# Feed-forward groups 2 to 4: the first product in three bf16 passes over exact parts of its input, inputs turned one step sooner

## The chip, the cores and the metric

One NeuronCore of a Trainium2 chip runs the whole program. The metric is the device time in microseconds of one execution. The kernel before was timed in 3 runs.

## What is computed

The input x is 16 images of 96 channels of 16 by 16 pixels, f32. The reference, cut to what matters:

```python
x = x + depthwise_conv_11x11(group_norm(x))                  # stage A
t = to_tokens(x)                                              # 16 x 256 tokens x 96 channels
t = t + attention(layer_norm(t))                              # 6 heads of 16, causal, rotary
t = t + ffn(layer_norm(t))
x = from_tokens(t)

def ffn(x, W1, b1, W2, b2):          # W1: 384 x 96, W2: 96 x 384
    h = bitlinear(x, W1, b1)
    h = gelu(h)                      # exact
    return bitlinear(h, W2, b2)

def bitlinear(x, W, b):
    Wb = sign(W - mean of its fifth of the rows)             # 5 row groups, the rest stays 0
    y = x @ Wb.T + b
    for g in range(5):               # 5 groups of 3 images; image 15 stays 0
        gamma = max(abs(y[g]))
        y[g] = clip(y[g] * 128 / (gamma + 1e-5), -128 + 1e-5, 128 - 1e-5)
    return y
```

Each group of 3 images (768 tokens) has one maximum over all of its hidden values and one over all of its outputs, and nothing behind a maximum can be scaled before it is known.

## The kernel before, in words

The program is written by hand, engine by engine: each engine's function lists its instructions in the order in which they are issued, and semaphores hold an instruction until others are done. There is no scheduler. An engine takes its instructions strictly in that order, so whatever stands behind a waiting instruction waits too.

Stage A (normalisation, convolution, projection to q, k, v) fills the first third. Then `step_b(n)` runs the attention, one image per step on every engine. The part of a step that matters here is on VectorE: `normalise_o`, a first row maximum (`maxima(n + 3, 0)`, L1028), `add_attention`, a second one (`maxima(n + 3, 1)`), and at the end of the step whatever small work on the feed-forward weights and statistics is due (`weight_sums`, `centre_w1`, `centre_w2`, `second_stats`).

The feed-forward stage begins inside the last steps with group 0 and then runs a loop over n = 1 to 4, in which all engines work on neighbouring groups. For a group g the work is this. GpSimd normalises the 768 tokens (`second_rstd`, L502, and `second_norm`, L511 and L514) into `x2_ring`, two groups deep. TensorE turns them to channel-major with six transposes (`transpose_x2`, L1567), part 0 (512 tokens) and part 1 (256 tokens). ScalarE copies each part from PSUM to `x2t_ring` (`channel_major`, L726); a row of ones below it carries the bias. TensorE makes the first product, three blocks of 128 hidden values for each part (`first_product`, L1583), f32, in two instructions each. VectorE reduces each block to its maximum (`largest_hidden`, L1141), and over `hidden_partial` (L1148), TensorE's `hidden_row` (L1590), `hidden_top` (L1154) and TensorE's `hidden_all` (L1595) every partition gets the group's maximum; `hidden_bounds` (L1132 to L1135) makes the clip limits, `clip_hidden` (L1182, L1187, L1191) clips, and ScalarE's `gelu` (L737) scales and applies the GELU. TensorE makes the second product (`second_product`, L1710), ScalarE adds the bias (`output`, L744), VectorE takes the output's maximum (`output_max`, L1196), and over `output_row` (L1742), `output_top` (L1206), `output_all` (L1746) and `output_bounds` the limits of the output come out. GpSimd clips (`limit_output`, L535), TensorE turns the residual (`residual`, L1731), and VectorE scales and adds (`scaled_output`, L1237), after which SyncE stores.

In round n TensorE issues the first product of group n, with the residual and the output maximum of group n - 2 between its blocks, then the second product of group n - 1 with the hidden maximum of group n and the transposes of group n + 1 between its blocks. ScalarE's round is output(n-1) part 0, channel_major(n+1) both parts, output(n-1) part 1, gelu(n) both parts. GpSimd's list behind the last attention step is: rstd and norm of group 3, rstd and norm of group 4, then the clips of the outputs of groups 0 to 4. Both parts of groups 2 to 4 are turned in the same PSUM bank (7), so part 1 waits until part 0 has been copied:

```python
def channel_major(g, part):
    act.wait_ge(s_x2t, 2 * g + part + 1)
    wait(act, s_f1, 2 * HC * (g - 1))
    n = SPANS[part].stop - SPANS[part].start
    nc.scalar.copy(x2t_ring[0:C, g % 2, SPANS[part]], bank[0:C, x2_bank(g, part), 0:n]).then_inc(s_x2c, 1)
```

## Time and profile before

| | us |
|---|---|
| median of 3 runs | 260.1 |
| the three runs | 256.66, 260.1, 261.04 |
| the profiled execution's own time | 258.36 |
| its span, first to last instruction | 256.6 |
| TensorE busy over the span | 230.8 (90%) |
| VectorE busy | 200.4 (78%) |
| ScalarE busy | 139.4 (54%) |
| GpSimd busy | 104.6 (41%) |

Durations and start times below come from one profiled execution and are microseconds from the span's start. An instruction's duration overlaps the next one's start where they are pipelined, so what an instruction costs on its engine is the distance between two starts. `[x <-ENGINE name Lnn]` at a row's end is idle time of the engine before that row and what ended it. PE is TensorE, DVE VectorE, ACT ScalarE, POOL GpSimd.

### The profile page before, as it was taken

The numbers are of one execution on the slowest core, as the hardware profiler recorded it, in microseconds if no ns is written. First come the engines' busy times: TensorE is split into PE (matmuls) and PEld (weight loads), VectorE is DVE, ScalarE is ACT, GpSimd is POOL, SyncE is SP. The second block draws the span as 40 slices with busy tenths as digits, with TensorE's granted clock in tenths as the row PEclk, the third lists the DMA queues.
The fourth block names the chain that finished last, engine by engine and source line by source line (L and its number), as shares of the span: only waits on it lengthen the run. The fifth ranks groups of instructions, "written<-read, shape, count | busy, mean of one in ns | idle before, by whom it ended". The sixth has DMA issues, their size and how long they took to land.

```text
span 256.6 us, 5459 instructions
## 1 busy us (share of the span) xinstructions
PE 230.8 (90%) x1864; PEld 176.8 (69%) x1864; DVE 200.4 (78%) x530; ACT 139.4 (54%) x324; POOL 104.6 (41%) x125
## 2 busy tenths in 40 slices
PE   7779989999999768789999998898998899999981
PEld 7679879899899645567877776676765545545450
DVE  3888988899896985677867777777485978888965
ACT  0351466586565466546876667667747524516250
POOL 2201358557556546433542224467365404010101
PEclk9799999999999999979999999999999999999995
DMA  3990000000699990443443545410000000101103
GB/s 100 251 318 1 0 0 3 1 0 4 103 115 118 119 102 0 84 95 76 86 103 94 94 97 95 92 32 4 0 3 1 3 0 0 46 12 37 46 0 107
DMA packets 24188, 15.68 MB, mean 61 GB/s; under 512 B 3069, under 2 KB 23522, under 8 KB 24162
## 3 DMA queue, kind: packets, MB, share of 16 engines
q1 hardware_dynamic: 22560, 14.06, 30.8%
q10 hardware_dynamic: 1602, 1.29, 2.2%
q8 instruction: 15, 0.25, 0.4%
q14 instruction: 11, 0.09, 0.2%
HBM read 4.26 MB, written 1.57 MB: 23 GB/s over the span
## 4 chain that ended last, share of the span: by engine, by line
PE 65%; DVE 19%; DMA 5%; issue 4%; ACT 2%; SPq 2%; POOL 1%; DVEq 0%; ACTq 0%
PE bank L1351 11%; PE bank L1583 7%; PE bank L1710 7%; PE bank L1461 6%; PE bank L1526 5%; DVE nmax L1028 5%; PE bank L1373 4%; PE bank L1464 4%; DVE xs_ring L891 3%; PE bank L1494 3%; PE bank L1362 3%; DMA stack<-nmax_t 3%; PE bank L1529 2%; DMA cst<-in_const 2%; PE bank L1475 2%
## 5 line engine op out<-in xcount | busy, mean ns | idle before, releaser
L1028 DVE TENSOR_REDUCE nmax<-bank 128x3 f32<-128x384 f32 x64 | 45.5, 752 | 20.6 <-PE bank L1464 20.5
L671 ACT ACTIVATE pt_ring<-bank 128x384 f32<-128x384 f32 x96 | 42.0, 491 | 20.2 <-PE bank L1496 19.6
L483 POOL TENSOR_SCALAR_AFFINE_SELECT pt_ring<-pt_ring 128x512 f32<-128x512 f32 x48 | 31.6, 660 | 49.8 <-ACT pt_ring L671 49.5
L1351 PE MATMUL bank<-xs_ring,toep 128*128 128x192 f32 x256 | 46.6, 328 | 1.0 <-DVE xs_ring L891 1.0
L1351 PEld LDWEIGHTS bank<-xs_ring,toep 128*128 128x128 f32 x256 | 41.8, 190 | 2.5 <-issue 1.2
L1461 PE MATMUL bank<-stack 96*128 96x128 bf16 x192 | 31.7, 250 | 4.3 <-DVE nmax L1028 3.0
L1464 PE MATMUL bank<-mask,ident 128*128 128x128 bf16 x192 | 31.6, 223 | 0.0
L450 POOL TENSOR_TENSOR parts<-rest_ring,parts 96x512 bf16<-96x512 f32 x16 | 18.7, 1171 | 22.3 <-ACT parts L603 22.3
L1461 PEld LDWEIGHTS bank<-stack 96*128 96x128 bf16 x192 | 18.6, 99 | 10.4 <-issue 6.4
L1494 PE MATMUL bank<-stack 97*128 97x256 bf16 x96 | 23.2, 277 | 1.3 <-DMA stack<-nmax_t 1.1
L1710 PE MATMUL bank<-parts,w_b 128*96 128x512 f32 (+1 forms) x60 | 23.1, 492 | 0.2 <-ACT parts L737 0.2
L1583 PE MATMUL bank<-parts,w_b 97*128 97x256 f32 (+1 forms) x60 | 23.2, 500 | 0.0
L443 POOL TENSOR_TENSOR rs_ring<-qk_ring,cst 128x384 f32<-128x384 f32 x16 | 18.1, 1134 | 5.4 <-ACT qk_ring L587 5.3
L1526 PE MATMUL bank<-pt_ring,v_ring 128*32 128x256 f32 x192 | 20.0, 387 | 0.0
L1496 PE MATMUL bank<-stack 97*128 97x128 bf16 x96 | 19.4, 220 | 0.0
L1464 PEld LDWEIGHTS bank<-mask,ident 128*128 128x128 bf16 x192 | 19.0, 99 | 0.2
L744 ACT ACTIVATE parts<-bank,b_s 96x512 f32<-96x512 f32 (+1 forms) x10 | 5.8, 575 | 23.6 <-PE bank L1710 23.4
L1373 PE MATMUL bank<-wa,lt_ring 96*128 96x288 f32 x64 | 18.5, 412 | 0.0
L587 ACT COPY qk_ring<-bank 128x384 f32<-128x384 f32 x16 | 7.7, 479 | 19.0 <-PE bank L1373 19.0
L957 DVE TENSOR_TENSOR qr_ring<-rc_ring,rs_ring 128x384 f32<-128x384 f32 x16 | 14.3, 896 | 2.1 <-POOL rs_ring L443 1.5
L891 DVE TENSOR_TENSOR xs_ring<-bank,cw_bc 128x384 f32<-128x384 f32 x32 | 15.6, 554 | 0.5 <-PE bank L1341 0.5
L1141 DVE TENSOR_REDUCE amax<-bank 128x1 f32<-128x512 f32 (+1 forms) x23 | 14.3, 636 | 1.4 <-PE bank L1583 1.2
(153 smaller groups left out, 470.7 us busy)
## 6 DMA issues: line engine op xcount, KB each, us to landing
stack<-parts SPq DMA_DIRECT2D x96, 96.0 KB, 3.6
tok<-in_x_tok SPq DMA_DIRECT2D x4, 384.0 KB, 12.0
out<-xs_ring SPq DMA_DIRECT2D x4, 288.0 KB, 2.6
stack<-in_x ACTq DMA_DIRECT2D x2, 384.0 KB, 8.7
stack<-nmax_t SPq DMA_DIRECT2D x32, 1.5 KB
stack<-in_x SPq DMA_DIRECT2D x2, 192.0 KB, 4.5
stack<-in_x SPq DMA_DIRECT2D x1, 384.0 KB, 11.0
cst<-in_const SPq DMA_DIRECT2D x1, 384.0 KB, 11.0
```

The source lines that it names most:

```text
L483: nc.gpsimd.affine_select(out=v, in_=v, compare_op=ALU.is_ge, fill=0.0, base=0, pattern=[[0, 2], [0, 2], [1, P]], channel_multiplier=-1).t ...
L671: nc.scalar.activation(pt_ring[:, b % 2, h, :], bank[:, 3 + h % 2, 0:T + P], ACT.Exp, scale=float(HD) ** -0.5).then_inc(s_exp, 1)
L891: last = nc.vector.tensor_tensor(xs_ring[:, s, p].rearrange("p t b c -> p (t b) c"), src, w, ALU.mult)
L1028: last = nc.vector.tensor_reduce(nmax[:, b % 2, k:k + 3], bank[:, 0:3, first:first + (t + 1) * P], op=ALU.max, axis=AX.X, negate=True)
L1351: last = nc.tensor.matmul(dst, w, xs_ring[:, s, p, k].rearrange("p b c -> p (b c)"), start=(k == 0 and p == 0), stop=(k == NT - 1 and p == ...
L1373: last = nc.tensor.matmul(bank[:, 5 + t, 0:3 * C], lt_ring[:, n0 % 2, (2 * u + t) * P:(2 * u + t + 1) * P], wa[:], start=True, stop=True)
L1461: nc.tensor.matmul(bank[:, h % 3, first:first + size], stack[0:KROWS, slot, h, 0, t * P:(t + 1) * P], stack[0:KROWS, slot, h, 1, 0:size], ...
L1464: last = nc.tensor.matmul(bank[:, h % 3, first + t * P:first + size], ident16[:], mask16[:], start=False, stop=True)
L1494: nc.tensor.matmul(bank[:, 3 + e, P:P + T], stack[0:KROWS + 1, slot, h, 1, 0:P], stack[0:KROWS + 1, slot, h, 0, :], start=True, stop=True)
L1526: nc.tensor.matmul(bank[rows, 7, g * T:(g + 1) * T], w, pt_ring[:, s, h, P:P + T], start=True, stop=False)
L1583: nc.tensor.matmul(dst, w1_b[:, k * P:(k + 1) * P], x2t_ring[:, g % 2, SPANS[part]], start=True, stop=True).then_inc(s_f1, 1)
L1710: m = nc.tensor.matmul(bank[0:C, 5 + part, 0:n], w2_b[:, k, :], h_ring[:, g % 2, k, SPANS[part]], start=(k == 0), stop=(k == HC - 1))
```

## The change

Groups 0 and 1 stay as they are. For groups 2 to 4 the f32 input of the first product is split into three bf16 parts that add up to it (`x2_16`): the rounded value, the rounded rest, and the rest of that. The sign weights, which are exact in bf16, are copied to `w1_16`, with three more rows that hold the bias in three bf16 parts against three rows of ones. TensorE makes each block in three bf16 passes (L1583 becomes three instructions).

The parts come from a chain over three engines: ScalarE copies each turned part twice, once to f32 and once to bf16 (`channel_major`); GpSimd subtracts (`rest_x2`, in place); ScalarE rounds the rest to bf16 (`middle_x2`); GpSimd subtracts again (`third_x2`). The first product of the group waits for all of it. To make room, the input of group n + 2 and no longer of n + 1 is turned in round n, and that of group 2 ahead of the loop. The bias parts are made by VectorE in attention steps 7 to 12 and placed by two transfers of SyncE, ScalarE makes `w1_16` in step 10, and VectorE writes the ones in step 5.

The diff, cut to its core:

```diff
+        w1_16 = sb("w1_16", [C + 3, HID], BF16)
...
+        x2_16 = parts[0:C + 3, n_used:n_used + 6 * GT].rearrange("p (s k n) -> p s k n", s=2, k=3)
...
+            sp.wait_ge(s_b1, 4)
+            for k in range(2):
+                sp.dma_start(w1_16[C + 1 + k:C + 2 + k, :], b1_parts[:, k, :]).then_inc(s_b1rows, 16)
...
+            def rest_x2(g):
+
+                pool.wait_ge(s_x2c, 2 * g + 2)
+                v = x2t_ring[0:C, g % 2, :]
+                nc.gpsimd.tensor_tensor(v, v, x2_16[0:C, g % 2, 0, :], ALU.subtract).then_inc(s_x2r, 1)
...
+            def third_x2(g):
+
+                pool.wait_ge(s_x2p1, g - 1)
+                nc.gpsimd.tensor_tensor(x2_16[0:C, g % 2, 2, :], x2t_ring[0:C, g % 2, :], x2_16[0:C, g % 2, 1, :],
+                                        ALU.subtract).then_inc(s_x2p2, 1)
...
             second_rstd(3)
             second_norm(3)
+            rest_x2(2)
+            third_x2(2)
             second_rstd(4)
             second_norm(4)
-            for g in range(QGROUPS - 2):
+            rest_x2(3)
+            third_x2(3)
+            limit_output(0)
+            rest_x2(4)
+            third_x2(4)
+            for g in range(1, QGROUPS - 2):
...
+                if n == 10:
+                    act.wait_ge(s_wsign, 1)
+                    nc.scalar.copy(w1_16[0:C, 0:QGROUPS * W1_ROWS], w1_b[0:C, 0:QGROUPS * W1_ROWS]).then_inc(s_w16, 1)
...
-                nc.scalar.copy(x2t_ring[0:C, g % 2, SPANS[part]], bank[0:C, x2_bank(g, part), 0:n]).then_inc(s_x2c, 1)
+                src = bank[0:C, x2_bank(g, part), 0:n]
+                last = nc.scalar.copy(x2t_ring[0:C, g % 2, SPANS[part]], src)
+                if g >= 2:
+                    last = nc.scalar.copy(x2_16[0:C, g % 2, 0, SPANS[part]], src)
+                last.then_inc(s_x2c, 1)
...
+            def middle_x2(g):
+
+                act.wait_ge(s_x2r, g - 1)
+                nc.scalar.copy(x2_16[0:C, g % 2, 1, :], x2t_ring[0:C, g % 2, :]).then_inc(s_x2p1, 1)
...
+            channel_major(2, 0)
+            channel_major(2, 1)
+            middle_x2(2)
             for n in range(1, QGROUPS):
                 output(n - 1, 0)
                 if n + 1 < QGROUPS:
-                    channel_major(n + 1, 0)
-                    channel_major(n + 1, 1)
+                    if n + 2 < QGROUPS:
+                        channel_major(n + 2, 0)
+                        channel_major(n + 2, 1)
                     output(n - 1, 1)
+                    if n + 2 < QGROUPS:
+                        middle_x2(n + 2)
...
+                    nc.vector.memset(w1_16[0:C, QGROUPS * W1_ROWS:HID], 0.0)
                     nc.vector.memset(w2_b[:, :, QGROUPS * W2_ROWS:C], 0.0).then_inc(s_wready, 1)
+                if n == 5:
+                    nc.vector.memset(x2_16[C:C + 3, :, 0, :], 1.0).then_inc(s_xrows, 1)
+                if n == 7:
+                    nc.vector.tensor_copy(w1_16[C:C + 1, :], w1_b[C:C + 1, :]).then_inc(s_b1, 1)
+                if n == 10:
+                    dve.wait_ge(s_b1, 1)
+                    nc.vector.tensor_tensor(b1_rest, w1_b[C:C + 1, :], w1_16[C:C + 1, :], ALU.subtract).then_inc(s_b1, 1)
+                if n == 11:
+                    dve.wait_ge(s_b1, 2)
+                    nc.vector.tensor_copy(b1_parts[:, 0, :], b1_rest).then_inc(s_b1, 1)
+                if n == 12:
+                    dve.wait_ge(s_b1, 3)
+                    nc.vector.tensor_tensor(b1_parts[:, 1, :], b1_rest, b1_parts[:, 0, :], ALU.subtract).then_inc(s_b1, 1)
                 if n in (8, 9, 13):
                     second_stats({8: 0, 9: 1, 13: 2}[n])
...
-                    wait(pe, s_out, 2 * (g - 3) + 1)
+                    wait(pe, s_out, 2 * (g - 4) + 1)
...
-                nc.tensor.matmul(dst, w1_b[:, k * P:(k + 1) * P], x2t_ring[:, g % 2, SPANS[part]],
-                                 start=True, stop=True).then_inc(s_f1, 1)
+                if g < 2:
+                    nc.tensor.matmul(dst, w1_b[:, k * P:(k + 1) * P], x2t_ring[:, g % 2, SPANS[part]],
+                                     start=True, stop=True).then_inc(s_f1, 1)
+                    return
+                pe.wait_ge(s_x2p1, g - 1)
+                pe.wait_ge(s_x2p2, g - 1)
+                for piece in range(3):
+                    rows = slice(0, C + 3 if piece == 0 else C)
+                    last = nc.tensor.matmul(dst, w1_16[rows, k * P:(k + 1) * P], x2_16[rows, g % 2, piece, SPANS[part]],
+                                            start=(piece == 0), stop=(piece == 2))
+                last.then_inc(s_f1, 1)
...
-                    pe.wait_ge(s_x2c, 2 * min(g + 3, QGROUPS))
+                    pe.wait_ge(s_x2c, 2 * min(g + 4, QGROUPS))
...
+            transpose_x2(2, 0)
+            transpose_x2(2, 1)
+            pe.wait_ge(s_w16, 1)
+            pe.wait_ge(s_xrows, 1)
+            pe.wait_ge(s_b1rows, 32)
             for n in range(1, QGROUPS):
...
-                if n + 1 < QGROUPS:
-                    transpose_x2(n + 1, 0)
+                if n + 2 < QGROUPS:
+                    transpose_x2(n + 2, 0)
...
                 second_product(n - 1, 1, 0)
                 second_product(n - 1, 1, 1)
-                if n + 1 < QGROUPS:
-                    transpose_x2(n + 1, 1)
+                if n + 2 < QGROUPS:
+                    transpose_x2(n + 2, 1)
                 second_product(n - 1, 1, 2)
```

What stands on GpSimd behind the last attention step, before (L502 and L511 to L514 are rstd and norm of a group, L535 and L542 the clips of the outputs):

```order
L514 TENSOR_TENSOR xs_ring<-xs_ring,ln_rstd 128x576 [waits s_x2m]
L502 TENSOR_TENSOR ln_rstd<-ln_var,mhalf 128x6 [waits s_l2var]
L511 TENSOR_TENSOR xs_ring<-tok,ln_mean 128x576 [waits s_x2t,s_l2rstd]
L514 TENSOR_TENSOR xs_ring<-xs_ring,ln_rstd 128x576 [waits s_x2m]
L535 TENSOR_SCALAR parts<-parts,lim 96x768 [waits s_sc2] x3
L542 TENSOR_SCALAR parts<-parts,lim 96x256 [waits s_sc2] x2
```

and in the changed kernel (L564 is `rest_x2`, L569 `third_x2`, L518 rstd, L527 and L530 norm, L551 and L558 the clips):

```order
L564 TENSOR_TENSOR parts<-parts 96x768 [waits s_x2c]
L569 TENSOR_TENSOR parts<-parts 96x768 [waits s_x2p1]
L518 TENSOR_TENSOR ln_rstd<-ln_var,mhalf 128x6 [waits s_l2var]
L527 TENSOR_TENSOR xs_ring<-tok,ln_mean 128x576 [waits s_x2t,s_l2rstd]
L530 TENSOR_TENSOR xs_ring<-xs_ring,ln_rstd 128x576 [waits s_x2m]
L564 TENSOR_TENSOR parts<-parts 96x768 [waits s_x2c]
L569 TENSOR_TENSOR parts<-parts 96x768 [waits s_x2p1]
L551 TENSOR_SCALAR parts<-parts,lim 96x768 [waits s_sc2]
L564 TENSOR_TENSOR parts<-parts 96x768 [waits s_x2c]
L569 TENSOR_TENSOR parts<-parts 96x768 [waits s_x2p1]
L551 TENSOR_SCALAR parts<-parts,lim 96x768 [waits s_sc2] x2
L558 TENSOR_SCALAR parts<-parts,lim 96x256 [waits s_sc2] x2
```

The rest and third of group 2 now stand ahead of the rstd and norm of group 4, those of group 3 ahead of the first output's clip, and those of group 4 ahead of the second's.

TensorE at the seam to the loop, before (the last block of group 1's first product, then the second product of group 0):

```order
L1583 MATMUL bank<-parts,w_b 128x512 [waits s_clip1,s_x2c]
L1710 MATMUL bank<-parts,w_b 96x512 [waits s_h,s_o,s_on]
L1590 MATMUL bank<-ident,gmax 1x128 [waits s_gm1]
L1710 MATMUL bank<-parts,w_b 96x512 [waits s_h]
L1595 MATMUL bank<-top,ones 128x1 [waits s_top1]
```

and in the changed kernel, where L1651 is the first product, L1634 the transposes, L1786 the second product, L1666 `hidden_row` and L1671 `hidden_all`:

```order
L1651 MATMUL bank<-parts,w_b 128x512 [waits s_clip1,s_x2c]
L1634 MATMUL bank<-ident,xs_ring 96x128 [waits s_x2,s_x2c,s_o,s_on]
L1634 MATMUL bank<-ident,xs_ring 96x128 x3
L1634 MATMUL bank<-ident,xs_ring 96x128 [waits s_x2c,s_x2]
L1634 MATMUL bank<-ident,xs_ring 96x128
L1786 MATMUL bank<-parts,w_b 96x512 [waits s_b1rows,s_h,s_xrows,s_w16]
L1666 MATMUL bank<-ident,gmax 1x128 [waits s_gm1]
L1786 MATMUL bank<-parts,w_b 96x512 [waits s_h]
L1671 MATMUL bank<-top,ones 128x1 [waits s_top1]
```

Six transposes have come between the first product of group 1 and everything behind it; the two of part 1 wait for ScalarE's copies of part 0.

## Rows read from the trace of the kernel before

**Rows 1.** Busy time by engine in two stretches: one round of the loop, and the tail.

```profile
211.78:222.47 10.69, 10.64 (x43) 5.60 (x42) 9.25 (x22) 4.39 (x7) 3.15 (x3) 1.00 0.10 28
...
243.33:256.60 13.27, 6.80 (x32) 4.03 (x32) 7.99 (x23) 3.97 (x8) 1.64 (x2) 0.80 0.18 52
```

**Rows 2.** Chain of waits through the feed-forward stage: start, length, what.

```profile
226.33 1.49 PE bank L1583 x6
```

**Rows 3.** Timeline of VectorE in the round of 222.47 to 233.16.

```profile
223.18 0.42 DVE L1196 TENSOR_REDUCE amax<-parts 96x1 f32<-96x256 f32 x1 [0.78 <-ACT parts L744]
...
226.37 0.16 DVE L1132 TENSOR_SCALAR gmax<-bank 96x1 f32<-96x1 f32 x1 [0.19 <-PE bank L1746]
...
228.56 0.74 DVE L1237 SCALAR_TENSOR_TENSOR xs_ring<-parts,lim,bank 96x512 f32<-96x512 f32 x1
...
229.23 0.27 DVE L1154 TENSOR_REDUCE top<-bank 1x1 f32<-1x128 f32 x1
```

**Rows 4.** Timeline of TensorE at the seam and in round 2.

```profile
206.17 1.02 PE L1710 MATMUL bank<-parts,w_b 128*96 128x512 f32 x2
...
207.31 0.27 PE L1590 MATMUL bank<-ident,gmax 128*1 128x128 f32 x1
...
216.97 1.02 PE L1710 MATMUL bank<-parts,w_b 128*96 128x512 f32 x2
...
220.31 0.60 PE L1567 MATMUL bank<-ident,xs_ring 128*96 128x128 f32 x4
...
221.81 0.40 PE L1567 MATMUL bank<-ident,xs_ring 128*96 128x128 f32 x2
```

**Rows 5.** Timeline of ScalarE in round 2.

```profile
221.10 0.57 ACT L726 COPY parts<-bank 96x512 f32<-96x512 f32 x1
...
222.67 0.47 ACT L744 ACTIVATE parts<-bank,b_s 96x256 f32<-96x256 f32 x1
```

**Rows 6.** ScalarE's groups by line and shape (busy, mean ns).

```profile
L603 ACT CAST parts<-rest_ring 96x512 bf16<-96x512 f32 x16 | 9.9, 622 | 2.4 <-DVE rest_ring L923 2.3
...
L726 ACT COPY parts<-bank 96x256 f32<-96x256 f32 x5 | 1.9, 374 | 1.7 <-PE bank L1567 1.7
```

**Rows 7.** Timeline of GpSimd behind the last attention step.

```profile
204.55 1.33 POOL L502 TENSOR_TENSOR ln_rstd<-ln_var,mhalf 128x6 f32<-128x6 f32 x1 [3.16 <-DVE ln_var L1048]
...
211.66 1.15 POOL L511 TENSOR_TENSOR xs_ring<-tok,ln_mean 128x576 f32<-128x576 f32 x1 [5.79 <-PE bank L1567]
...
216.19 0.97 POOL L535 TENSOR_SCALAR parts<-parts,lim 96x768 f32<-96x768 f32 x1 [2.15 <-DVE lim L1135]
```

**Rows 8.** GpSimd's groups by line and shape.

```profile
L450 POOL TENSOR_TENSOR parts<-rest_ring,parts 96x512 bf16<-96x512 f32 x16 | 18.7, 1171 | 22.3 <-ACT parts L603 22.3
```

**Rows 9.** Timeline of VectorE in attention steps 5, 9, 10 and 11.

```profile
136.36 0.44 DVE L1018 TENSOR_REDUCE w_sum<-w_b 128x5 f32<-128x285 f32 x1
...
159.88 1.42 DVE L1028 TENSOR_REDUCE nmax<-bank 128x3 f32<-128x384 f32 x2 [1.39 <-PE bank L1464]
...
162.25 0.23 DVE L1055 RECIPROCAL rsum<-bank 128x12 f32<-128x12 f32 x1
...
166.30 1.42 DVE L1028 TENSOR_REDUCE nmax<-bank 128x3 f32<-128x384 f32 x2 [1.38 <-PE bank L1464]
...
171.99 1.42 DVE L1028 TENSOR_REDUCE nmax<-bank 128x3 f32<-128x384 f32 x2 [0.92 <-PE bank L1464]
```

**Rows 10.** VectorE's groups by line and shape.

```profile
L915 DVE TENSOR_TENSOR rc_ring<-qk_ring,cst 128x384 f32<-128x384 f32 x16 | 11.6, 726 | 1.0 <-ACT qk_ring L587 0.8
...
L796 DVE MEMSET parts<- 1x1536 f32 x1 | 1.3, 1338 | 1.2 <-PEq L1825 1.2
```

**Rows 11.** Timelines of GpSimd and of VectorE, one moment, and VectorE's L1135 without GpSimd.

```profile
197.01 0.64 POOL L483 TENSOR_SCALAR_AFFINE_SELECT pt_ring<-pt_ring 128x512 f32<-128x512 f32 x1 [1.68 <-ACT pt_ring L671]
...
197.16 0.50 DVE L1135 TENSOR_TENSOR lim<-gmax,clip_at 128x2 f32<-128x2 f32 x1
...
219.75 0.14 DVE L1135 TENSOR_TENSOR lim<-gmax,clip_at 128x2 f32<-128x2 f32 x1
```

More of the change, by code:

```diff
@@ L182, in build @@
         y2_ring = wide[0:C, 2 * n_h + 2 * GT:2 * n_h + 4 * GT].rearrange("p (s n) -> p s n", s=2)
+        n_used = 2 * (2 * n_h + 4 * GT)
+        x2_16 = parts[0:C + 3, n_used:n_used + 6 * GT].rearrange("p (s k n) -> p s k n", s=2, k=3)
+        n_used += 6 * GT
+        b1_parts = parts[C:C + 1, n_used:n_used + 2 * HID].rearrange("p (k n) -> p k n", k=2)
+        b1_rest = parts[C:C + 1, n_used + 2 * HID:n_used + 4 * HID].bitcast(F32)
         flat = xs_ring[:, :, :, :, :, :].rearrange("p s q t b c -> p (s q t b c)")
@@ L277, in build @@
         s_x2c = sem("s_x2c")
+        s_w16 = sem("s_w16")
+        s_b1 = sem("s_b1")
+        s_b1rows = sem("s_b1rows")
+        s_xrows = sem("s_xrows")
+        s_x2r = sem("s_x2r")
+        s_x2p1 = sem("s_x2p1")
+        s_x2p2 = sem("s_x2p2")
         s_f1 = sem("s_f1")
```

## The prediction

> **What bounds the kernel now.** I read the busy time by stretch first. In one round of the feed-forward loop (10.69 us) TensorE is busy for 10.64 and VectorE for 9.25, at a granted clock of 1.00, the 2.4 GHz level [rows 1]. The chain of waits names nothing but TensorE there: the six instructions of the first product's part 1 alone stand in it with 1.49 us [rows 2]. Read so far, every 0.1 us taken from the first product would be won. VectorE's timeline says otherwise. In a round it sits idle only where it waits for part 1 of the output, 0.78 us ahead of the row at 223.18, and 0.19 us ahead of the one at 226.37, with a short wait of about 0.25 behind 229.43 [rows 3]. From 223.18 to the end of `hidden_top` at 229.50 it works without a break but for the 0.19. Then TensorE takes over (`hidden_all`, the rest of the second product, transposes), then ScalarE's `output` part 1 at 222.67, then VectorE again at 223.18 [rows 3, 5]. That ring is as long as the round, 10.69, and no first product lies on it. So TensorE and VectorE are balanced to a few tenths, and a faster first product only makes TensorE wait for the maxima.
>
> **The first product.** Three blocks of 512 and three of 256 tokens for each group. The six part-1 instructions take 1.49 us for 3 blocks of 256 [rows 2], less 0.2 of the last one's latency 1.28, so 0.43 a block of 256 and 0.85 a block of 512. f32 in two instructions is four passes if a bf16 pass runs a column in half the time of an f32 instruction; then three passes save a quarter: 3 x 0.21 + 3 x 0.11 = 0.96 us a group, 2.9 over groups 2 to 4. By the ring above only VectorE's 0.19 and some 0.12 between `hidden_top` and `hidden_all` can be won in a round: 0.3 instead of 0.96.
>
> **The seam to the loop.** Before, the second product begins at 206.17 and `hidden_row` of group 1 at 207.31 [rows 4]. Now the four transposes of part 0 come first. A set of four takes 0.60 (row at 220.31), so they end at 206.77. ScalarE then copies and casts the part: 0.57 for the copy (221.10), which starts the cast 0.47 later, and 0.58 for the cast, so 207.85 [rows 5]. Part 1 could start 0.14 behind that, as 221.81 stands to 221.67 now, at 208.0, and the second product at 208.2, two us late. From there `hidden_row` comes at 209.1 instead of 207.31, 1.8 late.
>
> **GpSimd's list is what decides.** It is strictly in order, and four new subtractions of 96x768 are put ahead of work that others need. The trace has no such subtraction. The nearest: 96x512 with a bf16 operand takes 1.171 [rows 8], scaled by elements 1.76, or 1.6 with a fixed 0.2; the f32 one of 128x576 takes 1.15 [rows 7], scaled 1.53. From below, a one-operand operation on 96x768 takes 0.97 [rows 7]; from above I allow 2.3, the 1.76 and the 0.5 of a stall as in rows 11, which here would hit GpSimd. I take 1.65. ScalarE's cast of the rest, 96x768 from SBUF, is 0.62 for 512 [rows 6] plus 0.21 for 256 more: 0.85 with its handover. rstd and norm of a group are 1.33 and two times 1.15 and, with 0.15 of handovers, 3.8 us [rows 7].
>
> Now the walk, on the clock of the old trace. The transposes of part 1 end at 208.4 and ScalarE's two operations (0.37 by rows 6, 0.26 apart) at 209.05. Rest of group 2 to 210.75, cast to 211.65, third to 213.3. Only then come rstd and norm of group 4, which ran from 204.55 when VectorE's statistics were there [rows 7] but are queued behind now: to 217.1. Rest of group 3 to 218.8, cast to 219.65, third to 221.3, clip of output 0 (0.97) to 222.3. Two others wait for this. ScalarE has `gelu(1)` queued behind the cast, so the second product of group 1 starts at 221.25 instead of 216.97 [rows 4]; and VectorE wants the clipped output at 217.88 (a round before 228.56, rows 3) and has `hidden_top(2)` queued behind it. `hidden_top(2)` starts at 223.05 and ends at 223.3, and `hidden_all(2)` is 4.3 us late. That contains the 1.8 of the seam. In round 1 alone the clip of output 0 finished at 217.16 (216.19 plus 0.97, rows 7), 0.7 ahead of its need; that cover is gone.
>
> **Rounds 2 to 4.** In round 2 part 1 of the transposes waits for one more ScalarE operation (+0.5; it starts at 221.81 now, straight behind the copy), and `output` part 1 for a second one (+0.1): 4.9 us late at the row 223.18. VectorE's 0.19 falls away: 4.7. Then comes a wait of another kind. VectorE's small two-operand L1135 took 0.50 instead of 0.14 when GpSimd's L483 ran from 197.01 to 197.65: it ended with it [rows 11]. Now the limits of output 1 (226.6 plus 4.7, so 231.3) meet `third_x2(4)` (rest from 227.7, cast, third from 230.25 to 231.9): +0.5, 5.2 late. In round 3 nothing is turned any more: six transposes and the wait between them, 0.85, leave the ring, 4.2 late, 4.0 behind VectorE's 0.19, and 0.15 once more at `hidden_all(4)`: 3.85 us at the loop's end, carried to the last store.
>
> The Trainium skill, "GPSIMD Engine Reference", section "Elementwise — side-by-side cycle accounting", gives about 2.6 cycles an element for a two-input operation at 1.2 GHz; by an estimate from that page 768 elements are 1.66 us and the sum stays as it is. By a rate in proportion to the f32 row of 576 it would be 1.53, 0.5 less over the walk. No row decides between them.
>
> **The attention steps.** Without extra work a step takes 5.69 us (166.30 to 171.99). With `second_stats`, some 1.0 us of extra work between the maximum that starts at 159.88 and the reciprocal at 162.25, it takes 6.42 (159.88 to 166.30) [rows 9]. So 0.3 of what is added at a step's end is hidden and the rest is paid in full. Step 5 already has a reduction of 0.44 there (136.36) that uses this up. It gets the write of ones, 1536 elements in a partition: the f32 fill of 1536 took 1.338 [rows 10], and I take 1.2 paid; if bf16 fills went four times as fast it would be 0.3. Step 7 has `centre_w2` and gets a cast of 384 elements, one operand against L915's two: I take 0.3 (0.9 with a stall as in rows 11). Steps 10 and 12 get a two-operand subtraction of 384; the same size of L915 took 0.73 on average, some of them stalled [rows 10], and a third of it bounds it from below: I take 0.5, of which 0.2 is paid in step 10 and 0.45 in step 12, where TensorE waits for `normalise_o` as soon as it can run. Step 11's cast hides, ScalarE's copy in step 10 fits into its idle 0.4, SyncE's two transfers come when its list is empty. Sum 2.2 us, between 0.6 and 4.5.
>
> The Trainium skill, "VectorE: DVE Perf Modes", section "Zero memsets can be issued as uint32 (trn2)", says that a fill takes a cycle an element whatever the type, and only fills of zero can be widened; ones in bf16 would then cost what f32 did, and the sum above is kept rather than reduced by 0.9.
>
> **The sum.** 3.85 + 2.2 = 6.05 us. On the profiled execution (258.36, with a span of 256.6) that is 264.4. The median of the runs shown, 260.1, lies 1.7 above it; the forecast on it is 266.2, 2.3% more. A measurement of this kernel can tell about 2% from no change, here 5.2 us.
>
> **Rivals.**
> TensorE bounds throughout, as the chain of waits has it. Then 0.96 a round is won, the seam's 1.8 is eaten up by it in two rounds, and 2.9 remains in all, since the transposes only change their place: 257.2 with the attention's additions hidden as well, 259.4 with them. For it speaks 10.64 of 10.69 us busy, against it VectorE's 9.25. It decides from the point where VectorE gets through a round in 9.7 us and a subtraction takes no more than 0.97, the bound from below. Chance 0.08; even 2.9 is only 1.1% faster.
> The mild case: subtractions cost about 1.15, as if a norm's. The four of the walk save 2.0, it ends at 220.3, and the whole is 260.1 + 4.05 = 264.1, within 2%. If instead the fill of ones is cheap, 265.3. Chance 0.30.
> The forecast, 266.2 with 264.5 to 268: 0.50.
> The clock falls: TensorE now idles from 219 to 221.25, longer than anywhere in the loop before. In the tail, where it is busy for 6.80 of 13.27 us, the granted clock is 0.80 on average [rows 1]. A stretch at 1.2 GHz would double what TensorE does in it, some 2 us: 268.5. Chance 0.12.
>
> So faster by over 2% has 0.03, within 2% 0.43, slower 0.54 (half of the forecast's own range and a little more lies above 265.3, with the clock case). The range is 262.0 to 269.5.
>
> **What would show it.** Right: TensorE idle of over 1 us behind the first transposes, and of some 2 us ahead of the second product of group 1; GpSimd busy without a break from rest 2 to the first clip, 12 to 13 us, its subtractions at 1.6; VectorE waiting over 3 us for the clip of output 0; step 5 of the attention longer by 1.2; rounds 3 and 4 near 10 us. Wrong: no wait for that clip, first products back to back and rounds of 9.8, subtractions under 1.2, or a step 5 of unchanged length.

## The result, and the profile of the changed kernel

| us | before | changed |
|---|---|---|
| median of 4 runs | 260.42 | 273.62 |
| lowest, highest | 256.66, 261.04 | 269.53, 274.31 |
| profiled execution, its span | 258.36, 256.6 | 273.14, 271.4 |
| mean granted clock in it | 0.976 | 0.952 |

The changed kernel is slower: ratio 1.053, 95% interval 1.046 to 1.061, where the forecast was 1.023. All ratios with an interval here leave out runs in which TensorE's clock stayed low for longer; medians hold all runs.

In the feed-forward stage things stand nearly as forecast. GpSimd's and then VectorE's timeline in round 1 of the changed kernel (start, length, engine, line; L564 is `rest_x2`, L569 `third_x2`, L551 the clip of an output, L1202 the limits, L1304 `scaled_output`):

```profile
218.82 1.64 POOL L564 TENSOR_TENSOR parts<-parts 96x768 f32<-96x768 f32 x1 [9.36 <-ACT parts L767]
...
226.74 1.64 POOL L564 TENSOR_TENSOR parts<-parts 96x768 f32<-96x768 f32 x1
229.32 1.64 POOL L569 TENSOR_TENSOR parts<-parts 96x768 bf16<-96x768 f32 x1 [0.94 <-ACT parts L773]
230.94 0.98 POOL L551 TENSOR_SCALAR parts<-parts,lim 96x768 f32<-96x768 f32 x1
```

```profile
227.86 0.53 DVE L1202 TENSOR_TENSOR lim<-gmax,clip_at 96x2 f32<-96x2 f32 x1
...
231.96 0.74 DVE L1304 SCALAR_TENSOR_TENSOR xs_ring<-parts,lim,bank 96x512 f32<-96x512 f32 x1 [1.84 <-POOL parts L551]
```

A subtraction takes 1.64 us (forecast 1.65). From the rest of group 2 to the end of the clip GpSimd takes 13.1 us, as forecast, with two breaks of 0.94 for ScalarE's casts. VectorE's small two-operand L1202 ends with GpSimd's instruction (227.86 + 0.53, 226.74 + 1.64). VectorE waits for the clip, but for 1.84 us and not for the "over 3 us" that the prediction gave as a sign: it already comes later to that point, since part 1 of the output had kept it waiting 1.37 us ahead of 224.58 (0.78 before, [rows 3]) and L1202 took 0.4 longer. The surprise is on TensorE. Its timeline at the same place (L1786 second product, L1666 `hidden_row`), and behind the write of ones in the attention (L1575 the transposed maxima, L1593 the weighted values):

```profile
217.68 0.39 PE L1634 MATMUL bank<-ident,xs_ring 128*96 128x128 f32 x2 [1.25 <-ACT parts L767]
...
230.87 1.38 PE L1786 MATMUL bank<-parts,w_b 128*96 128x512 f32 x2 [2.21 <-ACT parts L784]
232.03 0.42 PE L1666 MATMUL bank<-ident,gmax 128*1 128x128 f32 x1
232.25 1.91 PE L1786 MATMUL bank<-parts,w_b 128*96 128x512 f32 x2
```

```profile
137.92 0.27 PE L1575 MATMUL bank<-ident,nmax 128*12 128x128 f32 x1 [1.71 <-DVE o_norm L1111]
...
138.71 0.63 PE L1593 MATMUL bank<-pt_ring,v_ring 128*32 128x256 f32 x6
...
139.41 1.09 PE L1593 MATMUL bank<-pt_ring,v_ring 128*32 128x256 f32 x6
```

The same six instructions take 0.63 us at 138.71 and 1.09 at 139.41: the clock fell between them. The second product that took 1.02 [rows 4] takes 1.91 at 232.25. The stretches of 4 us with the lowest granted clock between 136 and 236 (stretch, its length, TensorE's busy time and instructions, granted clock, DMA share, GB/s); outside this part, the clock is low at the start (9 to 13) and in the last 2 us:

```profile
136.00:140.00 4.00, 2.29 (x28) 0.92 0.39 94
140.00:144.00 4.00, 4.00 (x33) 0.50 0.48 55
144.00:148.00 4.00, 4.00 (x27) 0.50 0.44 101
148.00:152.00 4.00, 4.00 (x48) 0.80 0.29 52
...
188.00:192.00 4.00, 4.00 (x39) 0.68 0.01 1
...
208.00:212.00 4.00, 4.00 (x34) 0.62 0.02 4
...
232.00:236.00 4.00, 4.00 (x11) 0.64 0.26 74
```

These are four falls (read in steps of 1 us, each goes down to 0.50, the 1.2 GHz level), each behind an idle stretch of TensorE: 1.71 us ahead of 137.92, 1.52 ahead of 186.53, 0.90 ahead of 207.51, 2.21 ahead of 230.87. Not every such stretch is followed by one: behind 1.43 us ahead of 94.64 and 1.25 ahead of 217.68 the clock stays at 1.00. While the clock is at 0.50 TensorE is busy all the time: it has become the bound. In VectorE's timeline the write of ones and the second maxima behind it:

```profile
135.78 1.34 DVE L1154 MEMSET parts<- 3x1536 bf16 x1 [0.38 <-issue]
...
143.42 1.42 DVE L1081 TENSOR_REDUCE nmax<-bank 128x3 f32<-128x384 f32 x2 [1.39 <-PE bank L1531]
```

The second maxima start at 133.62, 143.42 and 151.77, periods of 9.80 and 8.35 us where the kernel before had 6.14 and 6.11. Three explanations were put to the test. Theory A: the additions make TensorE idle, and the clock's falls behind that are what the forecast lacks. Rivals: the additions cost only their own time (B), or the falls have nothing to do with idle stretches (E).

### The profile page after: what moved, and what is told of

Its sections match the earlier page's. It is cut to its first block, busy times and chain, and to the rows that moved or that the text cites. A ratio compares the mean times of both kernels' runs of the same rounds, so it can differ in the third digit from the quotient of the medians.

```text
span 271.4 us, 5539 instructions
## 1 busy us (share of the span) xinstructions
PE 237.2 (87%) x1882; PEld 180.1 (66%) x1882; DVE 204.9 (76%) x536; ACT 144.5 (53%) x334; POOL 115.0 (42%) x131
## 4 chain that ended last, share of the span: by engine, by line
PE 51%; DVE 23%; SPq 6%; issue 6%; POOL 5%; DMA 4%; ACT 4%; DVEq 0%; ACTq 0%; POOLq 0%
PE bank L1418 7%; PE bank L1593 7%; SPq L381 6%; DVE nmax L1081 5%; PE bank L1528 5%; PE bank L1786 4%; PE bank L1561 3%; PE bank L1440 3%; DVE xs_ring L944 3%; PE bank L1531 3%; PE bank L1596 3%; PE bank L1651 2%; DMA stack<-nmax_t 2%; DMA stack<-in_x 2%; PE bank L1542 2%
## 5 line engine op out<-in xcount | busy, mean ns | idle before, releaser
L1528 PE MATMUL bank<-stack 96*128 96x128 bf16 x192 | 32.5, 254 | 4.2 <-DVE nmax L1081 3.0
L1531 PE MATMUL bank<-mask,ident 128*128 128x128 bf16 x192 | 32.4, 225 | 0.0
L1786 PE MATMUL bank<-parts,w_b 128*96 128x512 f32 (+1 forms) x60 | 24.1, 516 | 2.4 <-ACT parts L784 2.4
L1561 PE MATMUL bank<-stack 97*128 97x256 bf16 x96 | 24.1, 286 | 1.0 <-DMA stack<-nmax_t 0.9
L1593 PE MATMUL bank<-pt_ring,v_ring 128*32 128x256 f32 x192 | 21.9, 421 | 0.0
L1563 PE MATMUL bank<-stack 97*128 97x128 bf16 x96 | 20.1, 226 | 0.0
L1786 PEld LDWEIGHTS bank<-parts,w_b 128*96 128x96 f32 x60 | 8.9, 169 | 7.1 <-issue 4.9
```

The source lines that it names most:

```text
L1528: nc.tensor.matmul(bank[:, h % 3, first:first + size], stack[0:KROWS, slot, h, 0, t * P:(t + 1) * P], stack[0:KROWS, slot, h, 1, 0:size], ...
L1531: last = nc.tensor.matmul(bank[:, h % 3, first + t * P:first + size], ident16[:], mask16[:], start=False, stop=True)
L1561: nc.tensor.matmul(bank[:, 3 + e, P:P + T], stack[0:KROWS + 1, slot, h, 1, 0:P], stack[0:KROWS + 1, slot, h, 0, :], start=True, stop=True)
L1563: nc.tensor.matmul(bank[:, 3 + e, 0:P], stack[0:KROWS + 1, slot, h, 1, P:T], stack[0:KROWS + 1, slot, h, 0, P:T], start=True, stop=True).t ...
L1593: nc.tensor.matmul(bank[rows, 7, g * T:(g + 1) * T], w, pt_ring[:, s, h, P:P + T], start=True, stop=False)
L1786: m = nc.tensor.matmul(bank[0:C, 5 + part, 0:n], w2_b[:, k, :], h_ring[:, g % 2, k, SPANS[part]], start=(k == 0), stop=(k == HC - 1))
```

## The experiments

**e1, the ones written elsewhere.**

```diff
-                if n == 5:
-                    nc.vector.memset(x2_16[C:C + 3, :, 0, :], 1.0).then_inc(s_xrows, 1)
+            nc.gpsimd.memset(x2_16[C:C + 3, :, 0, :], 1.0).then_inc(s_xrows, 1)   # GpSimd, at the start
```

> The changed kernel, with the write of ones taken from the end of attention step 5 on VectorE to GpSimd's idle start. Theory A (the 1.34 us write delays TensorE, and the granted clock then falls to 1.2 GHz for some 10 us): both periods of the maxima behind it, 9.80 and 8.35 us now, return to about 6.1, so 5.9 us less, near 267.7. Rival B (only the write's own time is paid, the fall of the clock comes from something else in these steps): 1.2 us less, near 272.4, with the clock still at 0.50 after step 5.

Measured: median 267.91 (264.59 to 268.78), ratio to before 1.038 (1.020 to 1.056). The two periods are 6.15 and 6.11 us, as A has it and B does not. That the median also met A's 267.7 is in part luck. In the profiled execution (5.5 us shorter than the changed kernel's) the two periods give 5.9, the falls behind 1.52 us of idle ahead of 183.77 and 0.89 ahead of 203.43, stretches that it still has, did not come and gave 2.8, and falls at 14 to 21 and at 113 to 116, where the changed kernel's execution had only one at 9 to 13, took back 3.1.

**e2, the ones alone in the kernel before.**

```diff
+                if n == 5:
+                    nc.vector.memset(ones_rows, 1.0).then_inc(s_xrows, 1)
```

> The kernel before with nothing but the same write of ones, 3 partitions of 1536 bf16 values (one stretch instead of two of 768), at the end of attention step 5. Theory A: +5.9 us by the clock's fall in steps 5 and 6, near 266.3, ratio 1.023. Rival B: +1.2, near 261.6, ratio 1.005, clock at 1.00 there.

Measured: four runs between 258.25 and 266.51, median 263.08, between A's number and B's; no verdict. The profiled execution has periods of 9.72 and 8.43 us and a clock of 0.50 from 140 to 148; the run of 258.25 has a mean clock of 0.991. So the same write in the same place is followed by a fall in one execution and not in another. The kernel before has both kinds too: beside these kernels its runs were at 256.5 to 257.4 with a mean clock of 0.987, or at 260.6 to 262.9 with 0.970 or less. A is right about what the two periods lose when the clock falls (18.15 against 12.25, 5.9), but a fall comes in some executions only. The write's own price is between 258.25 - 257.4 = 0.9 and 258.25 - 256.47 = 1.8 us.

**e3, the seam alone.** Transposes and copies a step sooner, f32 throughout.

```diff
+            transpose_x2(2, 0)
+            transpose_x2(2, 1)
             for n in range(1, QGROUPS):
...
-                    transpose_x2(n + 1, 0)
+                    transpose_x2(n + 2, 0)
```

> The kernel before with the f32 first product kept and only the transposes and their copies a step sooner (group 2 ahead of the loop). No bf16, no subtraction. Theory: the seam makes the second product of group 0 some 1.5 to 1.8 us late and nothing but rounds without transposes gives back, so +1.0 to +1.8, 261.4 to 262.2, and the idle TensorE of about 1 us at the seam does not lower the clock. Rival C (any gap of over 1 us at the seam lowers the clock): +3 to +3.5, near 263.7.

Measured: ratio 1.0065 (0.998 to 1.015), seven runs, median 258.05. From the last second maximum to `hidden_row` of group 1 it takes 30.96 us against 29.64, 1.3 more; the rounds are 10.69, 10.70 and 10.15, so 0.5 comes back. TensorE's 0.76 us of idle time at the seam was followed by no fall in the profiled execution. The trace gives 0.8 us in all, just under the theory's 1.0 to 1.8; the ratio gives 1.7, but its interval (0.6 under to 3.9 over) tells little. Rival C spoke of a gap of over 1 us, which this kernel doesn't have; the changed kernel has it (1.25 us ahead of 217.68), and there the clock stays at 1.00.

**e4, the product alone.**

```diff
+                for piece in range(3):
+                    last = nc.tensor.matmul(dst, w1_16[0:C, k * P:(k + 1) * P], x2_16[0:C, g % 2, SPANS[part]],
+                                            start=(piece == 0), stop=(piece == 2))
```

> The kernel before with only the first product of groups 2 to 4 in three bf16 passes, all three over one rounded copy of the input (it leaves out the second and third part and the bias of these groups); ScalarE's copy writes bf16 instead of f32, order and everything else as before. Theory (VectorE closes the ring): a round is 0.3 us shorter, 0.9 in all, near 0.4% under the kernel before. Rival (TensorE bounds the loop, as the chain of waits says): 0.96 a round, 2.9 in all, 1.1% under it.

Measured: ratio 0.987 (0.972 to 1.002), fastest 255.09. `hidden_row` stands at 205.49, 215.75, 226.01 and 236.27: a round of 10.26 instead of 10.69, 0.43 each, 1.3 in three, and TensorE waits 0.28 for VectorE in every one. Ahead of the output's row it waits another 0.15. VectorE closes the ring, as the prediction said, but a round wins 0.43 and not 0.3. The ratio alone would also allow the rival's 1.1%; the rounds don't.

**e5, GpSimd's list made short.**

```diff
-                v = x2t_ring[0:C, g % 2, :]
+                v = x2t_ring[0:C, g % 2, 0:16]
```

> The changed kernel, with GpSimd's six subtractions of 96x768 cut to 96x16 and the third pass reading the second part again (it leaves out most of the splitting). Casts, passes, seam and order stay. Theory: GpSimd's list costs 2.6 us by the wait ahead of the second product of group 1 and another 1.4 by the fall of the clock that it causes at 231.7 to 234.5, so 4 us less, near 269.6. Rival D (the seam alone makes TensorE and VectorE late, the list hides): under 0.7 less, near 273.

Measured: median 270.93 (269.23 to 271.74), the profiled span 267.5 against 271.4, 3.9 less. `hidden_row` to `hidden_row` is 10.96, 10.96 and 9.50 us, against 13.22, 12.79 and 9.50 in the changed kernel; there is no wait ahead of the second product of group 1 and no low clock from 228 to 236. The three other falls are in its trace as in the changed kernel's, so the two traces can be compared. The median is only 2.7 less, the spans give the 4 of the theory. D is out.

**e6 and e7, TensorE kept busy, first try.**

```diff
+            def fill(count, at=7):
+                for k in range(count):
+                    nc.tensor.matmul(bank[:, at, 0:P], ident[:], ident[:], start=True, stop=True)
```

> The kernel before, with matrix products of the identity by itself, 128 columns f32 and 0.22 us each, put where TensorE idles: 3 in step 2, 2 each in steps 7, 8 and 11 ahead of the transposed maxima, 3 ahead of the last but one transpose of the attention's output. Their result is never read. Theory A (the granted clock falls behind idle stretches of TensorE, in some executions): the fall at 111.5 to 114.5 and others in the attention are gone, every run between 256.5 and 258, clock of 0.985 or more. Rival E (the falls have nothing to do with these stretches): the median stays at 260.9 or rises by up to 1, and the runs spread over 256.5 to 263 as before.

> The changed kernel, with the same products of the identity where it idles longest: as in the kernel before, and 7 in step 5, 6 in step 12, 5 between the transposes at the seam, 9 ahead of the second product of group 1. Theory A: no fall of the clock but in the tail; what stays is the change's own price, 6 to 8 us over 256.5, so 262.5 to 264.5. Rival E: within 1 us of the changed kernel, 273.6.

Measured: e6 median 257.66 where the kernel before beside it had 260.46, six of ten runs at 256.86 to 257.95, four still at 260.25 to 261.52: less than A said, more than E. e7 271.99 (270.75 to 273.02). Neither theory's number for e7, and its trace says why: its fillers stood a step too early. TensorE's timeline (L1538 is the filler):

```profile
134.07 1.78 PE L1538 MATMUL bank<-ident 128*128 128x128 f32 x14
...
143.24 0.27 PE L1580 MATMUL bank<-ident,nmax 128*12 128x128 f32 x1 [1.71 <-DVE o_norm L1111]
```

They ran where TensorE had work and the idle 1.71 us came whole a step later: the write at the end of VectorE's step 5 delays its step 6.

**e8, all additions moved, GpSimd and ScalarE reordered.**

```diff
             second_norm(3)
+            second_rstd(4)
             rest_x2(2)
+            second_norm(4)          # the subtraction of the mean only
             third_x2(2)
-            second_rstd(4)
-            second_norm(4)
+            second_scale(4)
...
-                        middle_x2(n + 2)
                     gelu(n, 0)
+                        middle_x2(n + 2)
```

`second_scale` is the second half of a group's normalisation, the multiplication.

> The changed kernel with all additions to VectorE's attention steps moved (ones written by GpSimd at the start, the four bias operations on GpSimd behind the selects of steps 5, 6, 7 and 12), group 4's statistics, and the first half of its normalisation, put ahead of the third parts of group 2 on GpSimd, and ScalarE's second cast of groups 3 and 4 behind the GELU of part 0. Nothing is left out. Theory: against the 267.9 of the kernel with the ones moved alone, the wait of 2.1 us and its fall of the clock of 1.4 ahead of the second product of group 1 go, and 0.8 of the bias steps: near 263.5, with the second product of group 1 waiting under 0.3. Rival F (VectorE's wait for the clip of output 0 holds the ring whatever the order): 266 or more.

Measured: median 263.31 (258.89 to 265.89), ratio 1.015 (1.006 to 1.024). The wait ahead of the second product of group 1 is gone, so rival F is out, and in its profiled execution so are steps 5 and 6 at a low clock (it has falls near 16, 114 and 203 instead). What is left are rounds 1 and 2 of 11.46 us each: part 1 of the transposes waits 0.52 for ScalarE's second operation on part 0, VectorE 1.37 for the output of part 1 (0.78 before, [rows 3]), and 0.5 goes to a stall of VectorE's small operation: L1214 takes 0.64 at 233.13 (0.14 without GpSimd, [rows 11]), ending with a subtraction of GpSimd that ran from 232.11 for 1.64.

**e9 and e10, those waits taken away, without and with fillers.**

```diff
-            return {(0, 0): 0, (0, 1): 1, (1, 0): 2, (1, 1): 1}.get((g, part), 7)
+            return {(0, 0): 0, (0, 1): 1, (1, 0): 2, (1, 1): 1, (3, 1): 5, (4, 1): 5}.get((g, part), 7)
...
                         channel_major(n + 2, 0)
-                        channel_major(n + 2, 1)
                     output(n - 1, 1)
+                        channel_major(n + 2, 1)
...
-            third_x2(3)
             limit_output(0)
+            third_x2(3)
```

> The changed kernel with its additions moved and GpSimd reordered as in e8, and three more waits taken away in the feed-forward loop: part 1 of the transposes of groups 3 and 4 goes to another PSUM bank, so it doesn't wait for ScalarE's two operations on part 0; ScalarE's output of part 1 stands ahead of its two operations on part 1; GpSimd's third parts stand behind the clips. At the seam part 1 stands behind the hidden_row. Nothing is left out. Theory (VectorE's ring, stretched by ScalarE's second operation and a port stall of 0.5, is what is left of the loss): rounds 1 and 2 fall from 11.46 us to 10.3, 2.3 us, and the seam gives 1; against e8 3 us less at the same clock, 256 to 257 where the clock doesn't fall. Rival (the second ScalarE operations hold elsewhere): under 1 us less.

> The same as e9, with products of the identity in TensorE's idle stretches, now in the steps where the trace has them: 2 more at the start, 3 each in the two gaps before the convolution, 4 each ahead of two waits in steps 0 and 1 of the attention (bank 6), 3 in step 2, 2 each in steps 9, 10, 11 and 13, 3 ahead of the last but one transpose of the attention's output. Theory A: all runs within 1 us of the fastest of e9, and their median 2 to 3 us under the median of e9. Rival E: same median and spread as e9.

Measured: e9 258.63 (257.29 to 259.89), e10 256.68 (256.58 to 258.74). Rounds 2 and 3 are 10.23 and 9.49 us, but round 1 stayed at 11.57, held, as it seemed, by the third parts of group 2; so e9's first two rounds gave 1.1 us of the 2.3 expected. The fillers (the products of the identity) took 2 us off the median; one run, 258.74, missed the 1 us that A allowed. The kernel before, beside them, had 256.57 to 256.87 in its better runs: e10 is level with it (ratio 1.002, 0.997 to 1.007), not under it.

**e11 and e12, fillers in the right steps.** The decisive pair: the changed kernel and the kernel before, both with TensorE kept busy. The lines below are e11 against e7; it has more fillers at the start and in steps 0 and 1, too.

```diff
-                fill({5: 7, 7: 3, 8: 2, 9: 2, 12: 6}.get(n, 0))
+                fill({6: 7, 9: 3, 10: 2, 11: 2, 13: 6}.get(n, 0))
```

> The changed kernel with the fillers of e7 put in the right steps: the write of ones at VectorE's step 5 makes TensorE wait in its own step 6 and the bias operation of step 12 in step 13, so 7 in step 6, 3 in 9, 2 in 10 and 11, 6 in 13, and those at the start and in steps 0 to 2 as in e10. Theory A: no fall of the clock behind the start and the change's own price remains, 263 to 265. Rival E: 270 to 274.

> The kernel before with the fillers of e10 (2 each in steps 9, 10 and 13). Theory A: all runs in one cluster at 256.5 to 257.5, the cluster at 260.3 to 261.5 that the first filling left is gone. Rival E: two clusters as before.

Measured: e11 264.84 (264.63 to 265.51), ratio to the kernel before 1.032 (1.030 to 1.034); e12 256.94 (256.83 to 259.23). The kernel before beside them had 256.57 to 256.87 four times and 261.88 to 263.09 three times. TensorE's timeline of e11 where the changed kernel was idle, and the same stretches as above:

```profile
135.77 1.78 PE L1538 MATMUL bank<-ident 128*128 128x128 f32 x14
137.64 0.27 PE L1580 MATMUL bank<-ident,nmax 128*12 128x128 f32 x1
```

```profile
140.00:144.00 4.00, 3.86 (x45) 1.00 0.26 43
144.00:148.00 4.00, 3.77 (x50) 1.00 0.72 115
```

The transposed maxima still come when VectorE lets them, but the clock stays at 1.00 from the start until only the last outputs are left (259 in e11, 251 in e12), where it falls in both. Only products whose result is never read were added, and 8.8 us are gone from the changed kernel: 264.63 to 265.51 against 269.53 to 274.31 (its four runs are those of the first measurement; it was not run again beside e11). E is out. In the kernel before there is less to gain. e12's median of 256.94 is that of the kernel before beside it, 256.87; what the fillers took away are the runs at 262 and 263, down to one at 259.23, and the mean falls from 259.1 to 257.5. A's "all runs in one cluster" missed by that one run.

**e13 and e14, the last of the chain, and the kernel before filled again beside it.**

```diff
+                for part in range(2) if g == 2 else [1]:
+                    pool.wait_ge(s_x2c, 2 * g + part + 1)
...
-                    pe.wait_ge(s_x2c, 2 * min(g + 4, QGROUPS))
+                    pe.wait_ge(s_x2c, 2 * min(g + 4, QGROUPS) - 1)
```

> e10 with the chain of group 2's parts shortened: GpSimd's first subtraction of group 2 in two pieces of 512 and 256 tokens, so it starts at ScalarE's cast of part 0, the second one directly behind it, and group 4's normalisation behind both; the residual waits for one cast less. Nothing is left out. Theory (round 1 of e10, 11.57 us, is held by the third parts of group 2, and round 2 by the residual's wait of 0.44): 1.0 to 1.5 us less than e10, 255.2 to 255.7 in the fast cluster. Rival G (VectorE's ring holds round 1 as well, the waits of TensorE there are slack): 256.5.

> The kernel of e12 again, beside e13 on the same chip, to compare the two with the clock kept: 256.9, with at most one run in five above 258. If e13 is under it by 1 us or more, three bf16 passes with their chain in the right places are worth something here; if not, they are worth nothing.

Measured: e13 256.07 (255.55 to 257.40), ratio to the kernel before 0.993 (0.989 to 0.998); e14 258.11 (256.90 to 259.38). Rounds of e13 are 10.84, 10.16 and 9.49 us where e10 had 11.57, 10.22 and 9.50, so round 1 was held by that chain, by 0.7 us, and G is out. The gain on e10 is 0.5 to 1 us, at or under the lower end of what was expected. e14 missed its own forecast: four of its six runs lie above 258, its median is that of the kernel before beside it (257.99), and its profiled execution has a fall at 97 to 101, behind 1.44 us of idle ahead of 94.59 and 0.97 ahead of 96.69, which have no filler. It did keep the highest run at 259.38 where the kernel before had 260.81, 261.68 and 262.41. e13 is the fastest kernel of the study that computes everything: its six runs are 1.35 us (lowest) to 2.0 (median) under e14's.

## Why the prediction was wrong

Two steps of the prediction failed. The clock was left out of the sum and put among the rivals at 0.12, as one fall of 2 us; it is the larger part of the miss. And the term "0.3 of what is added at a step's end is hidden" made the attention steps too cheap. The sum of the changed kernel's own costs was 6.05 us; e11 less e12 gives 7.9. The table sets the two traces, whose clock is kept up to the tail, against the terms.

| term | forecast | e11 against e12, start of maxima and `hidden_row` |
|---|---|---|
| step 5, ones | 1.2 | 8.07 - 6.14 = 1.9 |
| step 7, cast | 0.3 | 6.81 - 6.15 = 0.7, of which 0.2 comes back |
| step 10 | 0.2 | 6.24 - 5.68 = 0.56 |
| step 11 | 0 | 6.05 - 5.68 = 0.37 |
| step 12 | 0.45 | TensorE's wait 1.52 in the changed kernel, 0.67 in the kernel before (their traces without fillers): 0.85 |
| seam | 1.8 | (32.34 - 29.65) - 0.85 = 1.8, last second maximum to `hidden_row` of group 1 |
| rounds 1 to 3 | 2.05 | 34.03 - 32.07 = 2.0 |

- What bounds the loop: right. e4 shows VectorE's ring; the first product's own worth is 0.43 a round and not 0.3.
- The seam and GpSimd's list: right in mechanism and size, 3.85 forecast, 3.8 measured, subtractions at 1.64, the stall of VectorE's small operation forecast at 0.5 and 0.4 of it there twice (L1202 at 227.86, 0.53, and at 242.57, 0.48). The walk has a slip: 5.2 less 0.85 is 4.35 and not 4.2. Its last terms would then end at 4.0, not 3.85. The sign "over 3 us" for the clip doesn't follow from the walk either, which has VectorE ready at 219.7 and the clip at 222.3, 2.6 us.
- The attention steps: that VectorE's additions are paid there is right, the size is off, 2.2 forecast, 4.2 measured (3.34 from step 5 to step 12's maxima, and 0.85). The term that failed is "0.3 of what is added at a step's end is hidden", with step 12 as the only place where TensorE waits for `normalise_o`. In the traces 0.14 and 0.13 are hidden in steps 10 and 11 (0.56 paid for 0.70, 0.37 for 0.50), and steps 5 and 7 pay more than their instruction (1.9 for 1.34, 0.7 for 0.36). The reason is in TensorE's timeline of the changed kernel: it waits for `o_norm` (what `normalise_o` writes) in steps where, without an addition, it doesn't, 0.37 us ahead of 174.24 and 0.17 ahead of 180.29. What is added takes up VectorE's own idle time ahead of its first maxima (0.67 us ahead of 167.58 in e12, none ahead of 169.92 in e11), but TensorE, which got `o_norm` later, hands the second maxima over later (VectorE waits 1.39 and not 0.92 for them). A size was off besides: the subtraction was taken at 0.5, though rows 10 had 0.73 for its like. VectorE's timelines of e11, steps 10 and 11:

```profile
168.64 0.70 DVE L1159 TENSOR_TENSOR parts<-w_b,w 1x384 f32<-1x384 f32 x1
...
174.88 0.50 DVE L1162 CAST parts<-parts 1x384 bf16<-1x384 f32 x1
```

  In step 5 another 0.38 of idle time stands ahead of the write. One partition or 128 makes little difference: L915's 128x384 took 0.73 [rows 10], L1159's 1x384 takes 0.70.
- The step that lost the range was the clock. It stood among the rivals with 0.12, one fall of some 2 us at one place. In the medians, the changed kernel loses 273.62 - 264.84 = 8.8 us by falls and the kernel before 260.42 - 256.94 = 3.5, so 5.3 of the 13.2 us are the clock's and 7.9 the change's own. (The 3.5 hangs on that first measurement: beside e12 and e14 the kernel before had medians of 256.87 and 257.99, level with them. The 7.9 doesn't.) By place, the changed kernel's profiled execution against e11's: 18.15 - 14.18 = 4.0 us in the two periods behind step 5, 35.23 - 32.34 = 2.9 from the last second maximum to `hidden_row` of group 1, 26.01 - 24.53 = 1.5 in rounds 1 and 2; that is the 8.4 between their spans, 271.4 and 263.0. The place I named did fall, for 1.5 us of it. The prediction's own clue was the tail, and there a fall costs next to nothing: from `hidden_row` of group 4 to the end it is 17.08 us in the changed kernel, where the clock falls at 269, and 17.15 in e11, where it falls at 259, since TensorE has no work left there. Step 5 I had costed at 1.2 without asking what becomes of the clock behind a TensorE that idles for 1.7 us. The clue was there: the one low stretch shown of before was a stretch with an idle TensorE [rows 1], and the runs shown of before differed by 1.7%, which I took for noise around a median instead of for falls.
- The Trainium skill, "VectorE: DVE Perf Modes", section "Zero memsets can be issued as uint32 (trn2)", on fills: the trace agrees, ones in bf16 took 1.34 us for 1536, as f32 did [rows 10]. The Trainium skill, "GPSIMD Engine Reference", section "Elementwise — side-by-side cycle accounting": the estimate of 1.66 from it for the two-input subtraction agrees with 1.64.

Still open: what decides, in one execution and not in the next, that the clock falls behind an idle stretch of 1 to 2 us. TensorE idled 1.08 and 0.94 us near 110 in the kernel before and in the changed one alike; from 112 to 116 the clock was 0.65 in the first and 1.00 in the second. The wait of 1.52 us for `o_norm` was followed by a fall in the changed kernel and not in e1. The Trainium skill, "TensorE: Matmul & The Clock Gate", section "Part 1: The HAM clock gate", says that the gate's watch isn't aligned with a program's start, so that one kernel can meet it differently from run to run. The spread of one program is in line with it: e12 has 256.83, 256.86, 257.02 and 259.23, the last with a mean clock of 0.978 where the others have 0.992 to 0.994. No run here sets where the watch stands.

## What to carry to other kernels

Where TensorE is near its bound, a wait can cost twice: once its own length, and, in the executions in which the clock falls, once what the clock takes behind it. So small work that is added to another engine belongs where TensorE doesn't wait for it, and if it must wait, products whose result nobody reads, put right ahead of the waiting instruction, are cheap: e12's better runs (256.83 to 257.02) are within some 0.2 us of the unfilled ones beside them (256.57 to 256.87). They took 8.8 us off the changed kernel; off the kernel before they took its slowest runs, and 2.8 us (e6) or nothing (e12, e14) off its median. An engine's list is to be read for who waits behind each entry; with its parts in other places, the change that had cost 7.9 us was worth 0.9 to 2.0 (e13's median of 256.07 under those of e12 and e14; only e14 was run beside it).

## What the hardware showed that I had not expected

- Falls of the granted clock to 0.50 behind idle stretches of TensorE of 0.9 to 2.2 us in the middle of a busy kernel, in some executions and behind some of the stretches only. In the changed kernel the fall came at 139.4, 1.5 us after the work had begun again, and lasted until some 150.
- The same program runs at 256.6 or at 262 us, with mean clocks of 0.987 and 0.961 to 0.97; with fillers (e12) three runs of four at 256.9, and 0.993.
- VectorE's operations of 384 elements on one partition cost what they cost on 128: 0.70 and 0.73.
